# A graph network on one core: who waits for the compute engines' counters ahead of GpSimd's indirect DMAs

## The chip, the cores and the metric

One core of a Trainium2 chip. The metric is the device time of one execution in microseconds (us); times are medians of several runs. Engines: PE (TensorE), DVE (VectorE), ACT (ScalarE), POOL (GpSimd), SP (SyncE, which here only issues DMAs and waits).

## The reference

A graph with N = 50000 nodes of D = 128 features and E = 25000 directed edges, float32:

```python
h = relu(layernorm(x))
for W, b, cw, cb, a, g, be, blank in two_layers:           # sort convolution
    blank_p = W @ blank + b
    dense = up to 4 messages h[src] per node, the rest filled with blank_p
    srt = sort(dense, axis=1)                              # over the 4 slots
    o = a * h + einsum('nmd,m->nd', srt, cw) + cb
    h = h + batch_norm(o)                                  # statistics over all nodes
x = x + h
h = relu(layernorm(x))
for _ in range(5):                                         # gated graph convolution
    messages = h[col] @ W_msg.T + b_msg
    agg = segment_sum(messages, row, num_segments=N)
    h = gru(agg, h)                                        # gates r, z, n
x = x + h
```

## The kernel before, in words

Nodes are padded to NPAD = 50176, handled as NCH = 49 chunks of 1024 rows (8 per partition). Edges are sorted by target and stand as EC = 196 columns of 128. All five engines have their own program of one stage; they meet only at semaphores. Each indirect DMA (one column of 128 rows, gathered or scattered) is issued by POOL. All other DMAs of these stages are issued by SP, in the order of its program.

**Convolution** (`convolve`, once for each layer). 28 groups (NC) of seven columns (JC). POOL, in order: gather(i), seven DMAs into the ring M of four buffers (CR) (L721), then scatter(i - 3), seven DMAs out of the ring `ob` of three buffers (OR) (L729). For each group DVE masks and sorts the four slots (L818 to L847) and counts s_used and s_srt; ACT refills the blanks, moves the halo column and counts s_halo; PE mixes the sorted slots with 16 matmuls (L860) and counts s_mix; ACT adds the bias into `ob` (L784) and counts s_o. gather(i) waits for s_used and s_halo, scatter(i) for s_o. In layer 0 SP fills the second layer's output table with blank rows in 49 DMAs of 512 KB (`of`), released by s_used; in layer 1 SP has no part in the convolution.

**Statistics** (`statistics`). SP loads h (L887, 512 KB a chunk, four chunks ahead, waiting for nothing of the convolution) and the convolution's output (L893, once the scatters have landed, L892); DVE combines (L907), ACT squares (L938), PE sums over nodes with ones (L948). Beside it POOL scatters sorted columns for a later stage (L658, `pool_columns`), and waits there only for its own DMAs to land (L655).

**Second normalisation** (`apply1`). For each chunk SP loads h, o and x (L1106, L1107, L1109), three buffers deep, once DVE's L1228 three chunks back is done (s_x). DVE normalises (L2233 to L2237), adds (L1224, L1228), takes row statistics (L1235, L1240), and finishes the root and offset columns (L1209, L1211; s_row) into the ring a_r of four buffers (RR). POOL scatters the chunk to x_tab with eight DMAs (L1254) after s_row (L1250) and s_id (L1251: DVE's node number is written). Ahead of chunk NCH - 2 POOL waits for s_x and zeroes the last x buffer (L1249); SP waits for that (s_pad) before the last, partial x loads (L1111, L1113). ACT and PE compute the first step's messages in the same loop (L1129, L1137, L1144, L1156; L1174, L1181, L1184).

**Recurrent part.** Five steps; each has two halves of 49 jobs of 512 nodes. h=0: nodes without incoming edges, only their state part of the gates; beside it the gathers and the aggregation for the other half: for each group of four columns POOL gathers message rows into the ring G of four buffers (L1864), ACT builds selection matrices (L2051, L2056), PE multiplies (`tiles`, L1971; it counts s_sel), DVE adds to `agg` (L2113). h=1: nodes with edges, with the edge part of the gates (L1951, L2023). In each job DVE updates (L2164, s_d1; L2169; L2177, s_h) and evacuates the message tile (L2129, s_me) into one of two buffers m (r_m), PE makes it (`finish`, L1896). A gather waits for s_sel of four groups back (L1860). SP's order for a job: wait s_d1, load h of job k + 3 (L1753), loads and stores of the hidden parts made ahead (L1782, L1789, L1799), wait s_h, store h (L1836), store m of the job before (L1758 to L1764), in the second half of step FIN0 = 3 also the load of finished rows into a stage (L1773). In step FIN1 = 4 the first half has no jobs, only gathers, tiles and hidden parts; in the second half the result is not stored by SP: POOL puts it to the output out of r_m (L1878) after s_me. The finished half of step FIN0 is put out of the stage (L1871), where POOL waits only for the stage's load.

Of the kernel before, what the change touches and what calls it, by code (L numbers as in the profile page):

```python
# [28 lines left out]
CR = 4  # L29
# [49 lines left out]
def build(nc, x, src, dst, conv, gru, out):  # L79
# [39 lines left out]
    with ctx:  # L119
# [544 lines left out]
        def convolve(layer, c, banks, bank_read):  # L664
# [14 lines left out]
            s_sc = [stage_sem(f"{n}put{i}") for i in range(OR)]  # L679
            M0 = sb(n + "M_first", [P, 3, D], F32, c)  # L680
# [15 lines left out]
            def sync(sp):  # L696

                of = o_tab[1].rearrange("(c p t) f -> c p (t f)", p=P, t=RT)
                done = 0
                for i in range(NC):  # L700
                    sp.wait_ge(s_used, i + 1)
                    upto = NCH * (i + 1) // NC
                    for k in range(done, upto):
                        sp.dma_start(of[k], filled[1][:]).then_inc(s_fill, 16)
                    done = upto
# [8 lines left out]
            def gpsimd(pool):  # L714
                def gather(i):
                    if i >= CR:
                        pool.wait_ge(s_used, i - CR + 2)
                        pool.wait_ge(s_halo, i - CR + 2)
                    for q in range(JC):
                        j = JC * i + 3 + q  # L720
                        pool.indirect_dma_start(M[i % CR][:, 1 + q, :], None, h_tab[layer],  # L721
                                                bass.IndirectOffsetOnAxis(ap=gat_src[:, j:j + 1], axis=0)
                                                ).then_inc(s_m[i % CR], 16)

                def scatter(i):
                    pool.wait_ge(s_o, i + 1)
# [326 lines left out]
        def apply1(c, banks, spare, small, first_in):  # L1053
# [13 lines left out]
            s_pad = stage_sem("a1_pad")  # L1067
            s_w1 = stage_sem("a1_weights")
# [29 lines left out]
            def sync(sp):  # L1098
                sp.dma_start(w1[:], gru[0]).then_inc(s_w1, 16)
                for t in range(RT // 2):  # L1100
                    sp.dma_start(b1[:, t, :], gru[1].partition_broadcast(P)).then_inc(s_w1, 16)
                for i in range(NCH):
# [5 lines left out]
                    if i < NCH - 1:  # L1108
                        sp.dma_start(xb[k], xv[i]).then_inc(s_in[k], 16)  # L1109
                sp.wait_ge(s_pad, 1)  # L1110
                sp.dma_start(xb[kl][:, 0:full, :], x[m:m + full * P, :].rearrange("(t p) f -> p t f", p=P)  # L1111
                             ).then_inc(s_in[kl], 16)
                sp.dma_start(xb[kl][0:part, full, :], x[m + full * P:N, :]).then_inc(s_in[kl], 16)  # L1113

# [130 lines left out]
            def gpsimd(pool):  # L1245
                for i in range(NCH):
                    if i == NCH - 2:
                        pool.wait_ge(s_x, NCH - AR)
                        nc.gpsimd.memset(xb[kl], 0.0).then_inc(s_pad, 1)  # L1249
                    pool.wait_ge(s_row, i + 1)  # L1250
                    pool.wait_ge(s_id, 2 * i + 1)  # L1251
# [62 lines left out]
        with c:  # L1314
            banks = psum_pairs(c, "l1_ps")
            cv_vector, cv_tensor, cv_scalar, cv_gpsimd, _, _, cv_scattered, cv_free, cv_small = convolve(1, c, banks, None)
# [29 lines left out]
            @block.sync  # L1346
            def _(sp):
                st_sync(sp, cv_scattered)
                ap_sync(sp)
# [348 lines left out]
        s_op, s_oe = stage_sem("r_op"), stage_sem("r_oe")  # L1698
        c6 = ExitStack()
        with c6:  # L1700
# [46 lines left out]
            def _(sp):  # L1747
# [10 lines left out]
                def store_m(k):  # L1758
                    s, h, i = JOBS[k]
                    if h and s == FIN1:  # L1760
                        return
                    sp.wait_ge(s_me, k + 1)
# [4 lines left out]
                def staged(i):  # L1767
# [5 lines left out]
                    sp.dma_start(stg[i % 3][:].rearrange("p t f -> p (t f)"), msgv[2][i]).then_inc(s_sg[i % 3], 16)  # L1773

# [28 lines left out]
                for k, (s, h, i) in enumerate(JOBS):  # L1803
# [3 lines left out]
                    if turn and s == FIN1:  # L1807
                        for j in range(HALF + 1):
# [5 lines left out]
                            if j:  # L1814
                                store_ahead(ahead_at[s, j - 1])
                        load_kept(k)
# [26 lines left out]
                    if s == FIN0 and h:  # L1843
                        staged(i)
                for par in range(2):
# [5 lines left out]
            def _(pool):  # L1851
                nc.gpsimd.memset(zero[:], 0.0).then_inc(s_clr, 1)
                for s in range(STEPS):
# [3 lines left out]
                    for i in range(HALF):  # L1857
                        g = HALF * s + i
                        if g >= GR:
                            pool.wait_ge(s_sel, TQ * (g - GR + 1))  # L1860
# [13 lines left out]
                for i in range(HALF):  # L1874
                    k = job(FIN1, 1, i)
                    pool.wait_ge(s_me, k + 1)
# [391 lines left out]
```

## Time and profile before

| what | us |
|---|---|
| median of 3 runs | 6334.15 |
| lowest, highest | 6284.78, 6355.02 |
| span of the profiled execution | 6564.5 |

The profiled execution is one of its own, with the profiler on; its span is all of it, and it is 230 us (3.6%) longer than the median of the three unprofiled runs. Times in rows are microseconds from its start. "idle before" in square brackets is how long the instruction's engine had nothing to do ahead of it, with the instruction or engine that the profile takes for the one waited for; "issue" means that nothing is shown, "remote" that the releaser is not known. SPq are SP's DMA issues; PEld are PE's weight loads. "xN" is a count of like instructions that one row stands for.

### The profile page before, as it was taken

The numbers are of one execution on the slowest core, as the hardware profiler recorded it, in microseconds if no ns is written. First come the engines' busy times: TensorE is split into PE (matmuls) and PEld (weight loads), VectorE is DVE, ScalarE is ACT, GpSimd is POOL, SyncE is SP. The second block draws the span as 40 slices with busy tenths as digits, with TensorE's granted clock in tenths as the row PEclk, the third lists the DMA queues.
The fourth block names the chain that finished last, engine by engine and source line by source line (L and its number), as shares of the span: only waits on it lengthen the run. The fifth ranks groups of instructions, "written<-read, shape, count | busy, mean of one in ns | idle before, by whom it ended". The sixth has DMA issues, their size and how long they took to land. (4 is left out here: it accounts for less than half of the span.)

```text
span 6564.5 us, 61506 instructions
## 1 busy us (share of the span) xinstructions
PE 4257.9 (65%) x15022; PEld 2341.7 (36%) x15022; DVE 3845.9 (59%) x7518; ACT 2733.4 (42%) x5325; POOL 3376.4 (51%) x3399
## 2 busy tenths in 40 slices
PE   8944352602344754343577899789889978884586
PEld 5612121300121333232344455455445544442333
DVE  8965530397564255564466676667667756652265
ACT  6822210222222134343476654664465456433432
POOL 8766677046666434544665600640262056556666
PEclk9966676855666877677799999999999999997699
DMA  6722231694111585654476654664465456664444
GB/s 217 256 97 88 80 117 46 238 307 153 40 41 38 195 246 164 179 170 132 140 205 192 213 183 138 201 199 166 150 217 193 138 187 202 214 189 135 123 144 145
DMA packets 628093, 1062.87 MB, mean 162 GB/s; under 512 B 105048, under 2 KB 258158, under 8 KB 627740
## 3 DMA queue, kind: packets, MB, share of 16 engines
q1 hardware_dynamic: 498972, 818.46, 38.6%
q0 software_dynamic: 100544, 163.41, 9.0%
q10 hardware_dynamic: 28224, 77.08, 3.0%
q8 instruction: 126, 2.06, 0.1%
q14 instruction: 227, 1.86, 0.1%
HBM read 599.34 MB, written 464.81 MB: 162 GB/s over the span
## 5 line engine op out<-in xcount | busy, mean ns | idle before, releaser
L1864 POOL DMA_INDIRECT r_G<-msg_tab,srow x784 | 739.6, 943 | 1324.9 <-DMA msg_tab<-r_m 895.0
L860 PE MATMUL l_ps<-cv_V,cv_cwi 128*128 128x448 f32 x896 | 478.3, 702 | 916.7 <-ACT cv_ob L784 457.4
L1254 POOL DMA_INDIRECT x_tab<-a_r,node_pos x392 | 379.6, 968 | 514.7 <-DVE a_r L1211 246.7
L860 PEld LDWEIGHTS l_ps<-cv_V,cv_cwi 128*128 128x128 f32 x896 | 220.4, 253 | 1174.7 <-issue 1161.6
L2113 DVE TENSOR_TENSOR agg<-r_psS,agg 128x128 f32 x980 | 281.7, 287 | 514.7 <-DMA st_o<-o_tab 324.7
L729 POOL DMA_INDIRECT o_tab<-cv_ob,put_idx x392 | 387.7, 989 | 271.9 <-ACT cv_ob L784 147.8
L1945 PE MATMUL r_psR<-r_hin,whh 128*128 128x512 f32 x882 | 463.5, 608 | 27.3 <-ACT r_r L2066 11.4
L1896 PEld LDWEIGHTS r_psM<-wmsg,r_hnew 128*128 128x128 f32 x2744 | 355.8, 195 | 339.5 <-DVE r_hnew L2177 219.1
L1896 PE MATMUL r_psM<-wmsg,r_hnew 128*128 128x128 f32 x2744 | 384.0, 284 | 133.4 <-DVE r_hnew L2177 126.2
L721 POOL DMA_INDIRECT cv_M<-h_tab,gat_src x392 | 373.9, 954 | 119.5 <-issue 119.5
L1181 PE MATMUL l_ps<-a_bmsg,row 128*128 128x512 f32 x196 | 152.5, 871 | 429.3 <-ACT cv_M L1137 271.6
L907 DVE SCALAR_TENSOR_TENSOR st_o<-st_h,ab,st_o 128x1024 f32<-128x1024 f32 x98 | 125.9, 1285 | 507.9 <-DMA st_o<-o_tab 453.2
L784 ACT ACTIVATE cv_ob<-l_ps,cbb 128x896 f32<-128x896 f32 x56 | 56.4, 1007 | 817.5 <-remote 670.4
L948 PE MATMUL l_ps<-st_q,ones 128*128 128x512 f32 x384 | 213.0, 683 | 211.4 <-issue 181.1
L1917 PE MATMUL r_psR<-r_oin,whh 128*128 128x512 f32 x290 | 189.4, 740 | 245.5 <-issue 156.0
L658 POOL DMA_INDIRECT sort_tab<-pair,sort_at x196 | 195.6, 998 | 277.6 <-DVEq L1040 214.1
L1945 PE MATMUL r_psZ<-r_hin,whh 128*128 128x512 f32 x642 | 330.4, 596 | 11.9 <-issue 3.9
L818 DVE COPY_PREDICATED l_ps<-l_ps,cv_M 128x896 f32<-128x896 int32 x56 | 61.5, 1099 | 452.3 <-ACT cv_M L762 399.7
L2129 DVE TENSOR_TENSOR r_m<-r_psM,bmsg 128x512 f32<-128x512 f32 x343 | 235.7, 687 | 150.7 <-remote 80.3
L938 ACT ACTIVATE st_q<-st_o 128x1024 f32<-128x1024 f32 x98 | 103.3, 1056 | 514.5 <-remote 168.6
L1971 PE MATMUL r_psS<-r_sel,r_G 128*128 128x128 f32 x1960 | 293.0, 298 | 28.2 <-DMA r_G<-msg_tab,srow 17.7
L2051 ACT ACTIVATE r_dist<-iota_w,lrank 128x128 f32<-128x128 f32 x980 | 310.0, 390 | 0.0
(292 smaller groups left out, 11307.7 us busy)
## 6 DMA issues: line engine op xcount, KB each, us to landing
r_hin<-ht_tab SPq DMA_DIRECT2D x441, 256.0 KB
msg_tab<-r_m SPq DMA_DIRECT2D x392, 256.0 KB
ht_tab<-r_hnew SPq DMA_DIRECT2D x343, 256.0 KB
o_tab<-o_blank SPq DMA_DIRECT2D x98, 512.0 KB, 6.0
st_h<-h_tab SPq DMA_DIRECT2D x98, 512.0 KB
st_o<-o_tab SPq DMA_DIRECT2D x98, 512.0 KB
r_oin<-ht_tab SPq DMA_DIRECT2D x161, 256.0 KB
i_x<-x_tab SPq DMA_DIRECT2D x49, 528.0 KB
```

Of the source, the lines that this page charges most:

```text
L721: pool.indirect_dma_start(M[i % CR][:, 1 + q, :], None, h_tab[layer], bass.IndirectOffsetOnAxis(ap=gat_src[:, j:j + 1], axis=0)).then_inc( ...
L729: pool.indirect_dma_start(o_tab[layer], bass.IndirectOffsetOnAxis(ap=put_idx[:, j:j + 1], axis=0), ob[i % OR][:, q, :], None, bounds_check ...
L860: ins = nc.tensor.matmul(psO[:, h, 0:HW], cwi[m][:], V[i % 2][m][:, HW * h:HW * (h + 1)], start=m == 0, stop=m == 3)
L948: ins = nc.tensor.matmul(ps, w[:], t[:, 512 * q:512 * (q + 1)], start=i == 0 and q == 0, stop=i == NCH - 1 and q == 1, skip_group_check=True)
L1254: pool.indirect_dma_start(x2_tab, bass.IndirectOffsetOnAxis(ap=node_pos[:, j:j + 1], axis=0), rb[i % RR][:, t, :], None).then_inc(s_out[i ...
L1864: pool.indirect_dma_start(G[g % GR][:, q, :], None, msg_tab[s % 3] if s else first_tab, bass.IndirectOffsetOnAxis(ap=at, axis=0)).then_inc ...
L1896: ins = nc.tensor.matmul(psM[:, t, :], hnew[k % 2][:, P * t:P * (t + 1)], wmsg[:], start=True, stop=True)
L1945: ins = nc.tensor.matmul(ps, whh[:, g * D:(g + 1) * D], hin[k % 3][:], start=True, stop=not edges)
L1971: nc.tensor.matmul(psS[g % 2][:, q, :], G[g % GR][:, q, :], sel[g % 2][:, q, :], start=True, stop=True).then_inc(s_sel, 1)
L2051: nc.scalar.activation(dist[:, q, :], iota_w[:, 0:SW], ACT.Abs, bias=lrank[:, TQ * i + q:TQ * i + q + 1]).then_inc(s_di, 1)
L2113: nc.vector.tensor_tensor(agg[:, bass.ds(at[q], SW)], psS[g % 2][:, q, :], agg[:, bass.ds(at[q], SW)], ALU.add).then_inc(s_ev, 1)
L2129: nc.vector.tensor_tensor(mb[k % 2][:], psM[:], other, ALU.add).then_inc(s_me, 1)
```

## The change

Three kinds of edit, with two new semaphores for the convolution and one or two for the other stages. Ahead of its indirect DMAs POOL no longer waits for counters of DVE, ACT or PE; SP waits for these and increments a semaphore of its own for which POOL waits. In the convolution SP's loop runs over NC + OR rounds and its fills stand three groups later; it now runs in layer 1 too, ahead of the statistics' loads (in both layers these follow the whole loop). In `apply1` chunk i is passed on behind the loads of chunk i + 4, the last four behind or around the last two loads; the zeroing of the last x buffer stands one chunk earlier. In the recurrent part the pass for the gathers stands at the end of a job's work on SP, and `store_m` waits for s_me in the last half too and passes it on there.

```diff
             def sync(sp):
                 of = o_tab[1].rearrange("(c p t) f -> c p (t f)", p=P, t=RT)
                 done = 0
-                for i in range(NC):
-                    sp.wait_ge(s_used, i + 1)
-                    upto = NCH * (i + 1) // NC
+                for i in range(NC + OR):
+                    if CR <= i < NC:
+                        sp.wait_ge(s_used, i - CR + 2)
+                        sp.wait_ge(s_halo, i - CR + 2)
+                        sp.sem_inc(s_open, 1)
+                    if i >= OR:
+                        sp.wait_ge(s_o, i - OR + 1)
+                        sp.sem_inc(s_ready, 1)
+                    upto = NCH * max(0, i + 1 - OR) // NC if layer == 0 else 0
                     for k in range(done, upto):
                         sp.dma_start(of[k], filled[1][:]).then_inc(s_fill, 16)
                     done = upto
...
                 def gather(i):
                     if i >= CR:
-                        pool.wait_ge(s_used, i - CR + 2)
-                        pool.wait_ge(s_halo, i - CR + 2)
+                        pool.wait_ge(s_open, i - CR + 1)
...
                 def scatter(i):
-                    pool.wait_ge(s_o, i + 1)
+                    pool.wait_ge(s_ready, i + 1)
```

```diff
+                def send(i):
+                    sp.wait_ge(s_row, i + 1)
+                    sp.wait_ge(s_id, 2 * i + 1)
+                    sp.sem_inc(s_send, 1)
+
                 for i in range(NCH):
...
                     sp.dma_start(ob[k][:], ov[i]).then_inc(s_in[k], 16)
                     if i < NCH - 1:
                         sp.dma_start(xb[k], xv[i]).then_inc(s_in[k], 16)
+                    if i >= 4:
+                        send(i - 4)
+                send(NCH - 4)
                 sp.wait_ge(s_pad, 1)
...
                 sp.dma_start(xb[kl][0:part, full, :], x[m + full * P:N, :]).then_inc(s_in[kl], 16)
+                for i in range(NCH - 3, NCH):
+                    send(i)
...
             def gpsimd(pool):
                 for i in range(NCH):
-                    if i == NCH - 2:
+                    if i == NCH - 3:
                         pool.wait_ge(s_x, NCH - AR)
                         nc.gpsimd.memset(xb[kl], 0.0).then_inc(s_pad, 1)
-                    pool.wait_ge(s_row, i + 1)
-                    pool.wait_ge(s_id, 2 * i + 1)
+                    pool.wait_ge(s_send, i + 1)
```

```diff
             @block.sync
             def _(sp):
+                cv_sync(sp)
                 st_sync(sp, cv_scattered)
                 ap_sync(sp)
```

```diff
                 def store_m(k):
                     s, h, i = JOBS[k]
+                    sp.wait_ge(s_me, k + 1)
                     if h and s == FIN1:
+                        sp.sem_inc(s_send, 1)
                         return
-                    sp.wait_ge(s_me, k + 1)
...
+                def summed(g):
+                    sp.wait_ge(s_sel, TQ * (g + 1))
+                    sp.sem_inc(s_gopen, 1)
...
                             if j:
                                 store_ahead(ahead_at[s, j - 1])
+                            if 1 <= j < HALF:
+                                summed(HALF * s + j - 1)
...
                     if s == FIN0 and h:
                         staged(i)
+                    if h == 0 and i:
+                        summed(HALF * s + i - 1)
+                    if h and i == 0:
+                        summed(HALF * s + HALF - 1)
+                store_m(len(JOBS) - 1)
...
                         if g >= GR:
-                            pool.wait_ge(s_sel, TQ * (g - GR + 1))
+                            pool.wait_ge(s_gopen, g - GR + 1)
...
                 for i in range(HALF):
                     k = job(FIN1, 1, i)
-                    pool.wait_ge(s_me, k + 1)
+                    pool.wait_ge(s_send, i + 1)
```

## Rows read from the trace of the kernel before

**Rows 1.** The page's section 1: busy us (share of the span) and instructions by engine.
```profile
PE 4257.9 (65%) x15022; PEld 2341.7 (36%) x15022; DVE 3845.9 (59%) x7518; ACT 2733.4 (42%) x5325; POOL 3376.4 (51%) x3399
```

**Rows 2.** Windows: start:end, length, busy us (count) by engine; PEclk, DMA share, GB/s.
```profile
2370.00:3124.00 754.00, 307.75 (x1351) 216.99 (x1351) 438.12 (x1224) 308.85 (x680) 380.57 (x393) 0.70 0.57 167
3505.00:3810.00 305.00, 254.63 (x1114) 150.00 (x1115) 199.13 (x433) 198.61 (x416) 185.46 (x197) 0.97 0.66 205
3810.00:4090.00 280.00, 278.00 (x941) 148.09 (x940) 197.75 (x300) 130.64 (x200) 0.00 (x0) 0.99 0.46 155
```

**Rows 3.** Waits of POOL, whole span: tile, line <- releaser: us in total, times, longest.
```profile
POOL x_tab L1254 <- DVE a_r L1211: 246.7, 17, 16.1
...
POOL r_G L1864 <- DMA st_o<-o_tab: 219.3, 146, 4.2
...
POOL o_tab L729 <- ACT cv_ob L784: 147.8, 23, 8.5
...
POOL out_dram L1878 <- DVE r_m L2129: 69.6, 19, 21.7
```

**Rows 4.** Timeline, second convolution: start, us, instruction, [idle before <- releaser].
```profile
1709.53 9.19 PE L860 MATMUL l_ps<-cv_V,cv_cwi 128*128 128x448 f32 x16 [6.79 <-issue]
...
1735.10 0.94 POOL L721 DMA_INDIRECT cv_M<-h_tab,gat_src  x1 [0.30 <-issue]
1742.09 1.01 ACT L784 ACTIVATE cv_ob<-l_ps,cbb 128x896 f32<-128x896 f32 x1 [29.22 <-remote]
...
1743.90 1.01 POOL L729 DMA_INDIRECT o_tab<-cv_ob,put_idx  x1 [7.86 <-ACT cv_ob L784]
```

**Rows 5.** Waits in the stretch 911 to 1165, first statistics.
```profile
ACT st_q L938 <- remote: 148.7, 8, 21.4
```

**Rows 6.** Waits in the stretch 5600 to 5935, second half of the fourth step.
```profile
ACT r_r L2085 <- remote: 55.2, 12, 10.0
```

**Rows 7.** Timeline of one round of the second normalisation.
```profile
2436.05 0.17 DVE L1211 SCALAR_TENSOR_TENSOR a_r<-a_mv,a_r 128x8 f32<-128x8 f32 x1
...
2436.50 0.97 POOL L1254 DMA_INDIRECT x_tab<-a_r,node_pos  x1 [11.79 <-DVE a_r L1211]
2436.96 1.17 SPq L1109 DMA_DIRECT2D cv_high<-in_x_dram  x1
...
2437.77 0.97 POOL L1254 DMA_INDIRECT x_tab<-a_r,node_pos  x1 [0.30 <-issue]
```

**Rows 8.** Timeline of one period in the first half of a recurrent step.
```profile
3602.68 0.68 DVE L2177 TENSOR_TENSOR r_hnew<-r_psHN,r_d 128x512 f32<-128x512 f32 x1
...
3604.41 1.06 PE L1971 MATMUL r_psS<-r_sel,r_G 128*128 128x128 f32 x8
...
3607.66 0.29 DVE L2113 TENSOR_TENSOR agg<-r_psS,agg 128x128 f32 x1 [1.53 <-DMA st_o<-o_tab]
3607.80 0.94 POOL L1864 DMA_INDIRECT r_G<-first_tab,sorted  x1 [1.30 <-DMA st_o<-o_tab]
...
3608.66 0.68 DVE L2177 TENSOR_TENSOR r_hnew<-r_psHN,r_d 128x512 f32<-128x512 f32 x1
...
3609.37 0.32 SPq L1836 DMA_DIRECT2D ht_tab<-r_hnew  x1
...
3609.73 0.44 SPq L1764 DMA_DIRECT2D msg_tab<-r_m  x1
```

**Rows 9.** Timeline at the last puts.
```profile
6247.90 0.69 DVE L2129 TENSOR_TENSOR r_m<-r_psM,r_x 128x512 f32<-128x512 f32 x1 [1.65 <-DMA r_x<-x_tab]
...
6248.51 0.68 DVE L2164 TENSOR_TENSOR r_d<-r_hin,r_psHN 128x512 f32<-128x512 f32 x1
...
6249.42 1.01 POOL L1878 DMA_INDIRECT out_dram<-r_m,ids  x1 [21.67 <-DVE r_m L2129]
```

**Rows 10.** Timeline at the start of the second layer's convolution and statistics.
```profile
1548.66 4.94 SPq L887 DMA_DIRECT2D st_h<-h_tab  x4
...
2138.12 1.28 DVE L907 SCALAR_TENSOR_TENSOR st_o<-st_h,ab,st_o 128x1024 f32<-128x1024 f32 x1 [25.86 <-DMA st_o<-o_tab]
```

More of the change, by code:

```diff
@@ L679, in convolve @@
             s_sc = [stage_sem(f"{n}put{i}") for i in range(OR)]
+            s_open = stage_sem(n + "buffer_open")
+            s_ready = stage_sem(n + "rows_ready")
             M0 = sb(n + "M_first", [P, 3, D], F32, c)
@@ L1067, in apply1 @@
             s_pad = stage_sem("a1_pad")
+            s_send = stage_sem("a1_send")
             s_w1 = stage_sem("a1_weights")
@@ L1315, in build @@
             banks = psum_pairs(c, "l1_ps")
-            cv_vector, cv_tensor, cv_scalar, cv_gpsimd, _, _, cv_scattered, cv_free, cv_small = convolve(1, c, banks, None)
+            cv_vector, cv_tensor, cv_scalar, cv_gpsimd, cv_sync, _, cv_scattered, cv_free, cv_small = convolve(1, c, banks, None)
             st_vector, st_tensor, st_scalar, st_gpsimd, st_sync, st_in = statistics(1, c, banks, sort_tab, sort_at, pair,
@@ L1698, in build @@
         s_op, s_oe = stage_sem("r_op"), stage_sem("r_oe")
+        s_gopen, s_send = stage_sem("r_gather_open"), stage_sem("r_send")
         c6 = ExitStack()
```

## The prediction

> **What bounds the kernel now.** I read the page's busy times first: no engine is full over the span, PE is busy for 4257.9 us and POOL for 3376.4 of 6564.5 [rows 1], so the order of the work decides, stage by stage. The windows come next: in the first half of a recurrent step POOL issues 197 indirect DMAs and is busy for 185.46 us of 305, in the second half none in 280, with PE busy for 278.00 [rows 2]. Then POOL's waits, the rows that the change is aimed at: 147.8 us over 23 waits ahead of the scatters of both convolutions, 246.7 over 17 in the second normalisation, 219.3 over 146 ahead of the recurrent gathers, 69.6 over 19 ahead of the last puts [rows 3]. (The gathers' row names a DMA; by the code this wait is on PE's count of tiles, so I read the row as a misnamed releaser.)
>
> A wait on POOL's row costs time only if the one waited for was late for its own reasons. So I looked at one such place in time order. In the second convolution PE's group of 16 matmuls starts at 1709.53 and ends 9.19 later, at 1718.72. ACT, which waits for exactly that, starts its rows at 1742.09, after 29.22 of idle; POOL's last gather ended at 1736.04; POOL goes on at 1743.90 [rows 4]. For 23.4 us PE's increment was not seen, while POOL issued one DMA behind the other with 0.30 between; it came 6.05 us after POOL stopped. The three engines run in such cycles: a blind stretch as long as POOL's work in hand, then a few us in which everybody moves. The change can be of use only if this lateness comes from POOL's waiting on a compute engine's counter. Two stretches speak against that. In the first statistics stage POOL scatters too, and waits there for DMA counters only: ACT waits 21.4 us, eight times, 148.7 in all [rows 5]. In the second half of the fourth step POOL's puts wait only for a DMA's counter by the code, and ACT's wait for PE is still up to 10.0 us, 12 times [rows 6]. So the lateness goes with POOL's issuing, which the change leaves as it is: the same 7 or 8 or 4 DMAs in a row.
>
> One page would explain part of it by the way it is recorded. The Trainium skill ("Perfetto Trace Analysis", Per-engine timelines) says that TensorE's end is estimated from the instruction's size. The rows don't allow it for the bulk: ACT's start at 1742.09 is no PE end, and 23 us is more than twice the whole group [rows 4].
>
> **Convolutions.** Removed from POOL: two counter waits ahead of each gather from the fifth group on, one ahead of each scatter; added: one relayed wait for each. SP does nothing else in these stages but layer 0's 49 fills, so the relay costs one hop. A hop is seen in the recurrent part: DVE's add ends at 3609.34 and SP's transfer starts at 3609.37 [rows 8], 0.03 us. With the increment itself I take 0.08 for each of 23 waits: 23 × 0.08 = 2 us. Bounds: 0, and POOL's own way from ACT's end at 1743.10 to 1743.90 paid twice [rows 4], 23 × 0.80 = 18. The fills come three groups later and end with the convolution instead of before it; they feed only the second layer. The four loads of the statistics' first chunks are no longer issued early (1548.66, 4.94 us of SP [rows 10]) but behind SP's last relay, some 10 us before the first loads of the other operand; DVE starts on both at 2138.12 [rows 10]. That cover is thin, since 2 MB more are then in flight; I take 1.5 for each layer, +3, with bounds of 0 and 2 × 4.94 = 10.
>
> The same page speaks against any relay: a sequencer's semaphore step has a hidden tail, its propagation to the other engines is in no profiled window (the Trainium skill, "Perfetto Trace Analysis", Sequencer-only Instruction). "Advanced Engine Details and Errata", Network/Comms, in the Trainium skill gives 50 to 100 ns for a sequencer's read of a semaphore; 23 of those would be 1 to 2 us, by estimate the same sum.
>
> **Second normalisation.** SP passes chunk i on only after it has issued chunk i+4's three loads. At 2436.50 POOL starts on a chunk after 11.79 us of waiting for DVE's L1211 at 2436.05; SP's loads of that round run until 2436.96 + 1.17 = 2438.13 [rows 7]. The relay would open some 0.4 us after that, 2.0 later than now. That hits the rounds in which POOL waits: 17 × 2.0 = 34 us of POOL's time. Of chunk time it is less: eight DMAs of POOL are 8 × 1.27 = 10.2 us by the spacing of its starts (2436.50, 2437.77 [rows 7]), of 754/49 = 15.4 for a chunk [rows 2], and its tiles come free a whole chunk before DVE needs them. What it delays is when the blind stretch starts, and DVE gains the same time ahead of it. I take +2 for that and +3 for the end, where the last three relays stand behind the two last loads: +5. Bounds: 0 and 49 × 2.0 = 98. The memset's wait on DVE's counter stays, one group earlier.
>
> **Recurrent part, first halves.** SP relays behind the stores of the job: now the gather starts at 3607.80, L2177 ends at 3609.34, SP's two stores start at 3609.37 and 3609.73 and end by 3610.17 [rows 8]. So the relay opens 3610.17 − 3607.80 = 2.4 us later than POOL's wait does, 2.6 with a hop and an increment. PE reads this gather four periods behind the tiles that ended at 3605.47, from about 3605.47 + 4 × 5.98 − 1.06 = 3628.3 on, 20.5 us after its first DMA. The four DMAs take 4.7 to issue; if their landing took twice that again, 6 us would be left, and 2.6 of these go: nothing is late. What moves is the phase. PE's tiles end at 3605.47 and are added by DVE only at 3607.66, 1.16 us after POOL's fourth gather ended (3607.80 − 1.30 = 3606.50); the period is 3608.66 − 3602.68 = 5.98 [rows 8], against 280/49 = 5.71 in the half without gathers [rows 2]. If a later burst left PE's increments alone, 49 × 5 × 0.27 = 66 us would be gained; if it met the tiles' end 2.6 later in each period, DVE's slack of 35% of 5.98 (busy 199.13 of 305 [rows 2]) would take 2.1 of it, and 0.5 × 245 = 122 would be lost. Nearest to the row is that the cycle locks again to the end of the burst, one period being one burst: 0.
>
> **Last puts.** POOL starts at 6249.42, 0.83 after DVE's L2129 ended; SP's relay stands behind its wait for L2164, which ends at 6249.19 [rows 9], so 0.6 to 0.7 later. Both m buffers are then free later: 19 × 0.7 = 13 at most, 0 where PE and DVE are ahead; +2.
>
> **Sum:** 2 + 3 + 5 + 0 + 2 = +12 on the profiled execution, 6564.5 → 6576. That execution is 230 us longer than the median of the three runs, 6334.15, most likely in these same blind stretches, which differ from run to run; a term of 12 doesn't change by 3.6%. Forecast: 6334 + 12 = **6346 us**, own range 6300 to 6395. (About 1% is what a measurement of this kernel can tell from no change.)
>
> **Rivals.**
> A, faster: POOL's waiting on a compute counter is what holds increments back. For it: the waits of 147.8 and 246.7 are long and come just at these places [rows 3], and ACT's 29.22 ends when POOL's own wait begins [rows 4]. Price: 147.8 + 246.7 + 66 = 460 of the profile; half of it is 230, and gives 6104. Against it: rows 5 and 6. Chance 0.18. A weaker form, in which only the phase of the recurrent bursts is better: −66, 6268. Chance 0.12.
> B, slower: SP's order. [...] It decides where POOL's wait is on the path in each round, above all in the second normalisation: 49 × 2.0 = 98, 6432. For it: POOL there waits for DVE in 17 rounds [rows 3], and with SP in its loads at that moment [rows 7]. Against: eight DMAs are 10.2 of 15.4. The recurrent loss of 122 belongs here too (6456). Chance 0.24.
> C, the change doesn't do what it says: the memset still waits for a compute counter, and for the rest only the name of the counter changes; POOL waits as long, for the same engines' work at one remove. That is the forecast's own case: 0 to +12.
>
> **How the numbers follow.** Forecast 0.36 and C 0.10, together 0.46 within 1%. A 0.18 and its weaker form 0.12: 0.30 faster by over 1%. B: 0.24 slower by over 1%. Downwards the range reaches to 6150, which is the weaker form and 40% of A's 460 (6334 − 184); upwards over B's 6432, to 6440. Left out are A at its half and more, some 0.12, and B with both losses, 0.08.
>
> **What would show it.** Right: ACT's rows in the convolutions still wait above 20 us for PE, every third group; POOL's waits keep their sums of some 148 and 247 but name SP or an unknown; the period of the first halves stays at 5.98, with the gather 2.5 later in it; statistics start within 3 us as now. A would show as ACT starting within 1 us of PE's end while POOL issues, and as chunks of under 14.5 us. B would show as POOL's starts tied to the end of SP's loads, with chunks of 16.5 us and more. The forecast is wrong if a convolution stage changes by more than 10 us, or the second normalisation (754, rows 2) by more than 15.

## The result, and the profile after

| | us |
|---|---|
| before, median of 4 runs | 6344.59 (6284.78 to 6468.83) |
| after, median of 4 runs | 6600.64 (6589.59 to 6614.71) |
| ratio | 1.0425, 95% interval 1.0382 to 1.0467 |
| span of the profiled execution, before and after | 6564.5, 6608.5 |

The ratio leaves out runs more than 1.5% above a kernel's fastest (here the one of 6468.83, in one later session 14 of the 23 of the kernel before), so medians of all runs stand beside it, and it is these that I compare.

The change makes the kernel 256 us slower by these medians. The two profiled executions are only 44 us apart: the one of before happened to be 220 above its median, the one of after 8. So the profiles alone explain 44, and the rest had to be found in what differs between executions.

Windows of the profile after (start:end, length, busy by engine, PEclk, DMA share, GB/s): the second normalisation and the first half of a recurrent step.

```profile
2379.00:3065.00 686.00, 314.54 (x1335) 223.79 (x1336) 426.31 (x1219) 309.59 (x678) 381.59 (x393) 0.70 0.62 182
3455.00:3795.00 340.00, 273.02 (x1113) 172.05 (x1113) 199.46 (x433) 197.75 (x416) 185.42 (x196) 0.89 0.58 183
```

Against [rows 2] the normalisation is shorter (754 to 686) and the first half of a step longer (305 to 340), with the same work in it. Part of that is PE itself: its 1113 matmuls are busy for 273.02 us in place of 254.63, at a mean granted clock of 0.89 of full speed in place of 0.97. By POOL's first and last gather in the timeline the first three steps take 329.8, 335.4 and 332.8 us where they took 291.4, 292.2 and 291.8: 38.4, 43.2 and 41.0 more, 123 in all. The fourth is unchanged (298.9 before, 299.1 after). The sends of the normalisation, second to last chunk, spread over 653.0 instead of 725.0. The convolutions differ by 8 us each, downwards.

POOL's waits after, whole span:

```profile
POOL r_G L1895 <- SPq L1797: 368.1, 116, 7.7
POOL x_tab L1271 <- SPq L1113: 335.6, 19, 168.7
...
POOL o_tab L736 <- SPq L709: 134.2, 23, 7.9
```

The waits ahead of the scatters (134.2 over 23) and the puts (51.3 over 11) answer to [rows 3] with another name, as forecast. The gathers' are fewer and longer. In the first step they look so, before (3520 to 3790) and then after (3500 to 3780), each with the wait of ACT's gate in the same stretch:

```profile
POOL r_G L1864 <- DMA st_o<-o_tab: 51.0, 37, 3.4
...
ACT r_r L2066 <- PE r_psR L1945: 17.0, 38, 1.6
```

```profile
POOL r_G L1895 <- SPq L1797: 73.0, 21, 4.7
...
ACT r_r L2097 <- remote: 48.7, 16, 3.9
```

Half as many waits mean that the bursts pair up. I counted DMAs of POOL with at most 1.1 us between them as one burst: besides an opening one of 16 or 20, in each of the first three first halves the kernel before has 40 to 42 bursts of four gathers and one or two of eight, the kernel after 20 or 21 of eight and two to four of four. In the fourth step both kernels are mixed, 13 of eight and 18 of four before, 14 and 16 after, and take the same time. One pair of periods of the first step, after (timeline: start, us, instruction, idle before):

```profile
3599.15 1.02 PE L1976 MATMUL r_psR<-r_hin,whh 128*128 128x512 f32 x2
...
3600.83 0.95 POOL L1895 DMA_INDIRECT r_G<-first_tab,sorted  x1 [0.30 <-issue]
3603.55 0.69 ACT L2097 ACTIVATE r_r<-r_psR,brz 128x512 f32<-128x512 f32 x1 [3.76 <-remote]
...
3605.30 2.07 PE L1927 MATMUL r_psM<-wmsg,r_hnew 128*128 128x128 f32 x8 [4.27 <-DVE r_hnew L2208]
...
3606.40 0.95 POOL L1895 DMA_INDIRECT r_G<-first_tab,sorted  x1 [4.62 <-SPq L1797]
```

In [rows 8] a burst of four gathers ran over the end of the tiles, whose adds had room, and then POOL stopped for 1.3 us. Now eight gathers run from 3592.07 to 3601.78 with 0.30 between, and their last ones lie over PE's state part (3599.15 to 3600.17). ACT's gate, which waits for that, starts at 3603.55, 1.77 us after the burst's last DMA ended (3601.78), and the whole chain behind it (gate, h, PE's next m at 3605.30 after 4.27 of idle) is late. These eight matmuls then take 2.07 us, where the same eight took 1.16 in the kernel before (at 3603.41): the granted clock is 0.50 (1.2 GHz) from 3603.05 to 3609.87, after PE's idle stretch, and was 1.00 (2.4 GHz) all through this period before.

Not every increment of PE is late while POOL issues. In the kernel before PE's message tile ends at 3604.57, in the third DMA of a burst, and DVE starts on it at 3604.62; it is the tiles' end at 3605.47 that DVE sees only after the burst.

Second normalisation, after:

```profile
2437.27 0.17 DVE L1229 SCALAR_TENSOR_TENSOR a_r<-a_mv,a_r 128x8 f32<-128x8 f32 x1
...
2438.18 1.37 SPq L1122 DMA_DIRECT2D cv_high<-in_x_dram  x1
...
2439.90 0.97 POOL L1271 DMA_INDIRECT x_tab<-a_r,node_pos  x1 [4.12 <-SPq L1113]
```

POOL starts 2.46 us after DVE's columns are done (0.28 in [rows 7]), so the relay costs the 2.0 that was forecast, and yet the stage is shorter.

The second statistics stage, 2132 to 2379 in the profile before, has late increments too, which the prediction doesn't mention. ACT's squares wait there up to 20.7 us until POOL's stream of some 70 DMAs is issued:

```profile
ACT st_q L938 <- DMA st_o<-o_tab: 70.7, 7, 20.7
```

The profile after has the same (20.6), so the difference of the two profiles doesn't contain it.

### The profile page after: what moved, and what is told of

The parts are those of the page before. It is cut to its first block and busy times, and to the rows that moved or that the text cites. A ratio compares the mean times of both kernels' runs of the same rounds, so it can differ in the third digit from the quotient of the medians.

```text
span 6608.5 us, 61856 instructions
## 1 busy us (share of the span) xinstructions
PE 4337.0 (66%) x15022; PEld 2430.8 (37%) x15022; DVE 3841.8 (58%) x7518; ACT 2736.7 (41%) x5325; POOL 3379.1 (51%) x3399
## 5 line engine op out<-in xcount | busy, mean ns | idle before, releaser
L1927 PE MATMUL r_psM<-wmsg,r_hnew 128*128 128x128 f32 x2744 | 406.9, 296 | 188.6 <-DVE r_hnew L2208 183.2
L1927 PEld LDWEIGHTS r_psM<-wmsg,r_hnew 128*128 128x128 f32 x2744 | 388.8, 208 | 379.4 <-DVE r_hnew L2208 244.9
L736 POOL DMA_INDIRECT o_tab<-cv_ob,put_idx x392 | 388.6, 991 | 254.7 <-SPq L709 134.2
L2002 PE MATMUL r_psS<-r_sel,r_G 128*128 128x128 f32 x1960 | 328.5, 323 | 27.5 <-DMA r_G<-msg_tab,srow 16.6
L2002 PEld LDWEIGHTS r_psS<-r_sel,r_G 128*128 128x128 f32 x1960 | 305.5, 237 | 81.3 <-issue 59.8
L1938 PE MATMUL r_psHN<-r_hin,whh 128*128 128x512 f32 x560 | 314.1, 645 | 7.1 <-DMA r_hin<-ht_tab 7.1
```

The lines of the kernel that those rows point to most:

```text
L736: pool.indirect_dma_start(o_tab[layer], bass.IndirectOffsetOnAxis(ap=put_idx[:, j:j + 1], axis=0), ob[i % OR][:, q, :], None, bounds_check ...
L1927: ins = nc.tensor.matmul(psM[:, t, :], hnew[k % 2][:, P * t:P * (t + 1)], wmsg[:], start=True, stop=True)
L1938: nc.tensor.matmul(psHN[k % 2][:], whh[:, 2 * D:3 * D], hin[k % 3][:], start=True, stop=True).then_inc(s_hn, 1)
L2002: nc.tensor.matmul(psS[g % 2][:, q, :], G[g % GR][:, q, :], sel[g % 2][:, q, :], start=True, stop=True).then_inc(s_sel, 1)
```

## The experiments

Seven sessions, each kernel beside the kernel before on one chip. The chips fall in two kinds: on three the kernel before takes 5514 or 5515 us, on four 6421 to 6551 (and 6345 on that of the result). I call the second kind "late chips", for what the profile of e1 shows below. Each chip was seen in one session only, so "chip" here always means the chip in that session.

| experiment | edit | kernel before | median | ratio (95%) |
|---|---|---|---|---|
| e1_gather_only | gathers' relay alone | 5515 | 5512.7 | 0.9994 (0.9985 to 1.0004) |
| e2_norm_only | normalisation's relay alone | 5515 | 5510.4 | 0.9988 (0.9977 to 0.9998) |
| e3_conv_only | convolutions' part alone | 5515 | 5519.0 | 1.0009 (0.9999 to 1.0019) |
| e4_all_but_gather | all but the gathers' relay | 5515 | 5520.3 | 1.0006 (0.9996 to 1.0016) |
| e5_whole_again | the whole change | 5515 | 5523.1 | 1.0016 (1.0005 to 1.0026) |
| e6_gather_again | as e1 | 5515 | 5513.4 | 0.9998 (0.9989 to 1.0008) |
| e7_direct_late | later wait, no relay | 6421 | 6624.4 | 1.0311 (1.0270 to 1.0352) |
| e8_gather_third | as e1 | 6421 | 6585.7 | 1.0241 (1.0198 to 1.0284) |
| e9_all_but_gather_again | as e4 | 6551 | 6557.8 | 1.0149 (1.0087 to 1.0211) |
| e10_conv_again | as e3 | 6551 | 6596.8 | 1.0233 (1.0175 to 1.0290) |
| e11_h_late | h loads late, nothing else | 6518 | 6553.0 | none |
| e12_conv_h_early | e3 with early h loads | 6518 | 6453.8 | 0.9964 (0.9858 to 1.0070) |
| e13_norm_again | as e2 | 6518 | 6478.5 | none |
| e14_pause | stops beside the statistics | 6531 | 6419.6 | 0.9993 (0.9952 to 1.0035) |
| e15_pause_norm | e14 and e2 | 6531 | 6387.5 | 0.9978 (0.9950 to 1.0007) |
| e16_whole_pause | e14 and the whole change | 6531 | 6558.2 | 1.0232 (1.0179 to 1.0284) |
| e17_conv_stop | e15 and stops in the convolutions | 5514 | 5686.8 | 1.0315 (1.0301 to 1.0329) |
| e18_pause_norm_again | as e15 | 5514 | 5578.1 | 1.0116 (1.0101 to 1.0132) |

**The parts, one at a time (e1 to e6).** e1, the core of its edit:

```diff
-                            pool.wait_ge(s_sel, TQ * (g - GR + 1))
+                            pool.wait_ge(s_gopen, g - GR + 1)
```

with `summed` and its calls on SP as in the change; e2, e3 and e4 take the change's lines of their stages as they are.

> Of the change only the relay ahead of the recurrent gathers. Theory 1 (phase: the later burst of four gathers now runs while PE finishes what the gates wait for): nearly all of the loss is here, the first halves of steps 0 to 2 take 330 to 336 us instead of 292, and the time is 150 to 300 above the kernel before (ratio 1.025 to 1.047). Theory 2 (every relay costs, through SP's order): a third of the loss at most, ratio under 1.015.

> Of the change only the second normalisation's relay. Theory 1: that stage is faster, sends spread over 640 to 670 us instead of 725, ratio 0.985 to 1.000 (1.000 if the kernel before has its slow stage only in the profiled execution). Theory 2: slower, ratio above 1.005.

> Of the change only the convolutions' part. Theory 1: within 0.4% of the kernel before; the profile's convolutions differ by under 10 us each. Theory 2: slower by 0.5 to 1.5%.

> The whole change, but the recurrent gathers wait for PE's counter themselves again. Theory 1: the loss is gone, ratio 0.98 to 1.005, first halves of steps 0 to 2 at 292 us. Theory 2: most of the loss stays, ratio above 1.02.

> The whole change once more. The runs of its parts stood beside a kernel before of 5515 us, not 6344, and on that chip ACT starts 0.04 us after PE's end in the convolutions where it had waited up to 23 us. Theory 1 (the loss needs the late increments): where the kernel before takes about 5515, ratio 0.998 to 1.003; where it takes about 6340, ratio 1.03 to 1.05. Theory 2 (the parts add up to a loss only together, whatever the chip): ratio above 1.02 also at 5515.

> Only the recurrent gathers' relay, once more. Theory 1: at a kernel before of 5515 ratio 1.00 as in the first run of it; at 6340 ratio 1.03 to 1.05, with first halves of steps 0 to 2 of 330 us or more. If the loss at 6340 comes from the other parts instead, ratio 0.99 to 1.01 there.

All are within 0.2% of the kernel before, beside 5515 us. The whole change costs 8 us there. e1 missed what theory 1 said of it; e2, e3 and e4 lie within theirs, which says little on a chip that shows no loss at all; e5 came out as its theory 1 had it, so the chip decides. The profile of e1 shows what is absent on such a chip. Second convolution, PE's mixing and ACT's rows (timeline):

```profile
1467.15 9.33 PE L860 MATMUL l_ps<-cv_V,cv_cwi 128*128 128x448 f32 x16 [9.88 <-DVEq L847]
...
1476.52 1.01 ACT L784 ACTIVATE cv_ob<-l_ps,cbb 128x896 f32<-128x896 f32 x1 [7.53 <-PE l_ps L860]
```

and the first half of the first recurrent step (window):

```profile
2830.00:3077.00 247.00, 242.09 (x1112) 150.73 (x1112) 194.46 (x431) 200.44 (x415) 184.71 (x196) 0.98 0.79 252
```

ACT starts 0.04 us after PE's end, with POOL issuing its DMAs in the same 1.25 to 1.3 us rhythm; in [rows 4] it was 23.4. It is 0.04 in all 56 groups of both convolutions of e1, while 33 of the 56 in the kernel before are over 1 us, up to 27.8. A half step takes 247 us, not 305. So late increments come with the chip (or with how it was set up in that session), not with the kernel, and without them the whole change costs 0.16% (e5). The 0.04 also says that the modelled end of PE, which the prediction put aside with the Trainium skill's "Perfetto Trace Analysis", Per-engine timelines (TensorE's end is estimated from the instruction's size), is no source of the lateness.

**The relay or its moment (e7, e8), on a late chip.** e7 leaves the relay out and takes only its later moment:

```diff
                             pool.wait_ge(s_sel, TQ * (g - GR + 1))
+                            sb_, ib = divmod(g - GR, HALF)
+                            if sb_ < FIN1:
+                                kb = job(sb_, 0, ib + 1) if ib + 1 < HALF else job(sb_, 1, 0)
+                                pool.wait_ge(s_h, kb + 1)
+                                pool.wait_ge(s_me, kb)
```

> The kernel before, but each recurrent gather also waits, on GpSimd itself, for the h (s_h) and the m (s_me) behind which SyncE would pass it on; nothing is relayed. Theory 1 (phase): where the kernel before takes about 6340, this is as slow as the relay, ratio 1.03 to 1.05, since the burst of gathers starts as late in the job. Theory 3 (it is the relay itself, GpSimd waiting on SyncE's counter): ratio 0.99 to 1.01. Where the kernel before takes about 5515, both say 0.998 to 1.002.

> Only the gathers' relay, beside e7_direct_late on the same chip. Theory 1: the same ratio as e7_direct_late within 0.01, above 1.03 where the kernel before takes 6340. Theory 3: above 1.03 there, with e7_direct_late at 1.00. At 5515 both 1.00.

Ratios 1.0311 and 1.0241, the second below the 1.03 that was expected; in medians of all runs 204 and 165 us. The first halves of steps 0 to 2 take 349.8, 349.9 and 346.9 us in e7, 349.1, 352.0 and 350.1 in e8. Theory 3 falls: GpSimd waiting itself, on a compute counter, is as slow as the relay once it waits for the same moment. The gathers pair up in the same way, 21 bursts of eight in the first half step of both e7 and e8. POOL's waits in e7, 3400 to 3700:

```profile
POOL r_G L1869 <- DVE r_hnew L2182: 84.0, 19, 5.4
```

So it is the later moment that makes the pairs. Through which step it does was not isolated. The fourth step of e11, a run whose recurrent part is that of the kernel before, shows that it needs no relay: 17 bursts of eight there, and 331 us in place of 299.

**What the other parts do on a late chip (e9, e10).**

> The whole change but for the gathers' relay, in the hope of a chip on which the kernel before takes 6300 to 6450. There: theory 1 (the gathers' phase makes the loss, the normalisation's relay gains some 70): ratio 0.98 to 0.995, first halves at 292 us. Theory 4 (the convolutions' part tips the first statistics stage into its long form in every run: 281 us where a short one takes about 110): ratio 1.00 to 1.02. At a before of 5515: 1.000 to 1.002.

> Only the convolutions' part. Where the kernel before takes 6300 to 6450: theory 1 says ratio 0.995 to 1.005 and both forms of the first statistics stage in the runs, some 150 us apart; theory 4 says every run has the long form, ratio 1.015 to 1.03. At a before of 5515: 1.000 to 1.002.

The first halves of steps 0 to 2 are back at 291 to 294 us, so all of the recurrent loss belongs to the gathers. But e9 misses the 0.98 to 0.995 of theory 1, being slower than the fast half of the kernel before's runs, and all 6 runs of e10, the convolutions' part alone, lie above 6500 (median 6596.8), as theory 4 had it. In e10's profile the convolutions are as before (578.0 against 577.9 for the second, 567.4 against 572.5 for the first); the stretch between them, with the first statistics, takes 653, as in the profile before. The same stretch took 485 in e7. How it comes about is in the profile after; ACT's squares in the first statistics stage, each with its wait:

```profile
921.03 1.06 ACT L945 ACTIVATE st_q<-st_o 128x1024 f32<-128x1024 f32 x1 [2.38 <-issue]
927.17 1.06 ACT L945 ACTIVATE st_q<-st_o 128x1024 f32<-128x1024 f32 x1 [5.09 <-remote]
943.96 1.06 ACT L945 ACTIVATE st_q<-st_o 128x1024 f32<-128x1024 f32 x1 [15.73 <-remote]
966.36 1.06 ACT L945 ACTIVATE st_q<-st_o 128x1024 f32<-128x1024 f32 x1 [21.34 <-remote]
```

The wait starts at 2.38, climbs within a few chunks to 21.34 and stays there until POOL's stream of gathers is issued (L661 before, 196 DMAs). Some executions escape the climb: in e7 the wait stays at 3.6 and less through the same unbroken stream, and that is worth 168 us. In e8 the climb begins only after some 20 chunks, and the stretch takes 611. I call the ends a long and a short form of the stage.

The second statistics stage has them too. By its squares, first to last, it takes 219 to 229 us in six late traces (before, after, e7, e8, e9, e13) and 164 to 166 in six (e10, e11, e12, e14, e15, e16), some 60 less; on the other chips it takes 165. So the time of one execution depends on two stages, each with a form of its own.

On late chips 29 of the 57 runs of the kernel before lie above 6500 us (none of the four of the result); of the 18 of e9, e10 and e11, 17 do.

**Why it climbs more often (e11, e12).** e11 is the kernel before plus one line at the end of SP's convolution loop, and e12 is e3 with the four h loads issued ahead of the last three rounds:

```diff
+                sp.wait_ge(s_o, NC)
```

```diff
                     done = upto
+                    if i == NC - 1 and between:
+                        between(sp)
```

> The kernel before with one wait more: SyncE issues the first statistics stage's four h loads only after the last s_o, as the change does; no relay, fills as before. Theory 4a (the late h loads tip that stage into its long form): where the kernel before takes 6300 and more, every run long, above 6500. Theory 4b (it is not the loads but the rest of the convolutions' part, the late fills or the relay): both forms, a third to a half of the runs short, under 6500. At a before of 5515: 1.000 to 1.001.

> The convolutions' part of the change, but with the four h loads issued ahead of the last three relays and fills, where the kernel before has them. Theory 4a: both forms among the runs, as in the kernel before. Theory 4b: every run long, above 6500. At a before of 5515: 1.000 to 1.002.

e11: 5 of 6 runs above 6500. e12: 3 of 6, and 6 of 11 for the kernel before beside them. That leans to theory 4a (the late h loads), whose "every run" failed. Alone e11 proves little: in its session early loads give 9 of 17 above 6500. With the session of e9 and e10, late loads give 17 of 18 and early ones 16 of 28, which chance would make in under 1% of cases; but 12 of the 18 also have the relays and the late fills. So the late loads are the likelier cause and not a shown one, and through which step they tip the stage was not seen.

> Only the second normalisation's relay. Theory 1: where the kernel before takes 6300 and more, 50 to 75 us faster form for form (ratio 0.985 to 0.995), its sends spread over 650 to 685 us instead of 721 to 725. If that gain needs other parts of the change, ratio 1.00. At a before of 5515: 0.998 to 1.000, as measured there.

e13 has six runs from 6358 to 6554, median 6478.5 beside 6517.7 (39 less, where 50 to 75 was expected), and its sends spread over 656.3 us: the gain in the sends is real by itself, how much of it arrives can't be read from runs that scatter over 200. The traces say more. From the last scatter of the second convolution to the first recurrent gather, with the long form of the second statistics, it takes 1375, 1407 and 1397 us without this relay (before, e7, e8) and 1325, 1344 and 1378 with it (after, e13, e9); with the short form 1328 to 1333 without (e10, e11, e12, e14) and 1306 and 1303 with it (e15, e16). So some 25 us arrive beside the short form; beside the long one the traces scatter too much to tell.

**A short stop (e14 to e16).** In the column DMAs beside the statistics (`pool_columns`) every group of 14 now waits for the group before it:

```diff
+                if i >= 1 and first:
+                    pool.wait_ge(s_done[(i - 1) % 2], 16 * JG * ((i - 1) // 2 + 1))
```

> The kernel before, with a pause for GpSimd: in the column scatters and gathers beside the statistics (L658, L661) each group of 14 waits until the group before it has landed, so GpSimd stops for some 2 us after every 14 DMAs. Theory 5 (compute increments pile up while GpSimd issues without a gap, and a short stop lets them through): where the kernel before takes 6300 and more, no run has the long first statistics stage (no ACT wait above 18 us in it), all runs within 6250 to 6450, ratio to its short runs 0.97 to 1.00. Theory 6 (a stop that short clears nothing): both forms as before, and the pauses cost 10 to 40 us. At a before of 5515: 1.00 to 1.01, slower if anything.

> e14_pause with the second normalisation's relay: 45 to 75 us below e14_pause on a chip where the kernel before takes 6300 and more; at 5515 within 10 us of it.

> The whole change with the same pause. If theory 5 holds and the change's loss is the gathers' phase plus the long statistics stage, the second goes: 6400 to 6500 where the whole change alone has 6600, and e16 minus e15 is the recurrent part's 120 to 170. If the pause clears nothing, 6590 and more.

Theory 5 held: all 12 runs of e14 lie between 6391 and 6445, where the kernel before beside it has 13 of 23 above 6500. Same stretch, 911 to 1165, in the kernel before and in e14 (windows):

```profile
911.00:1165.00 254.00, 90.25 (x146) 36.69 (x147) 25.32 (x20) 19.02 (x18) 192.73 (x196) 0.66 0.25 75
```

```profile
911.00:1165.00 254.00, 170.35 (x392) 75.14 (x392) 140.40 (x119) 68.44 (x66) 171.24 (x160) 0.84 0.83 295
```

ACT makes 66 operations in it instead of 18. And where [rows 5] has eight waits of up to 21.4 us from an unknown releaser, the waits of e14 there are

```profile
ACT st_q L940 <- PE l_ps L950: 75.2, 32, 3.3
```

POOL's stops in it come to

```profile
POOL look L663 <- DMA look<-node_tab,src_at: 35.2, 10, 4.3
```

35 us of waiting, and 45 over the whole stage (13 stops, the longest 5.9). The stretch between the convolutions takes 536 us in e14, against 653 in the long form and 485 in the short one. The stops cost 51 beside the short form and save 117 beside the long. The second statistics stage, which has the stops too, is short in all three traces of e14 to e16. A stop waits until the DMAs have landed, so it ends POOL's issuing and its DMAs' traffic at once; which of the two holds the increments back wasn't separated. e15 takes 32 us less than e14, not the 45 to 75 expected: its sends spread over 673.9 instead of 723.4, but the first gather of the recurrent part comes only 24 us earlier after the convolution (1307.4 instead of 1331.6), as the stage's end follows another chain. e16 missed its 6400 to 6500 (all six runs lie above 6549). Against e15 it has the change's recurrent part and its convolutions' part: 6558.2 − 6387.5 = 171 us; first halves of 352.9, 353.8 and 351.7 against 291.9, 294.2 and 293.8, together 178.5. On this pair the gathers' later moment explains the whole difference, and it costs more for each half step than on the chip of the result (60 against 41).

e15 is the version to have on a late chip: 144 us (2.2%) below the kernel before's median of all runs. It is no faster than the fast runs of the kernel before (0.9978); what it gains is that no run is slow.

**What it costs elsewhere (e17, e18).** e17 adds the same kind of stop to the convolutions:

```diff
+                    if OR <= i < NC:
+                        pool.wait_ge(s_m[i % CR], 16 * JC * (i // CR + 1))
                     if i >= OR:
                         scatter(i - OR)
```

> e15_pause_norm with a stop in the convolutions too: ahead of each scatter GpSimd waits until the gather that it has just issued has landed, about 2 us in every 18. Theory 5: where the kernel before takes 6300 and more, ACT's waits of 29 us for PE in the convolutions fall under 12, the stop costs GpSimd 28 x 2 us in each layer and saves about as much: within 40 us of e18 either way. Theory 6 (there a short stop clears nothing): e18 plus 80 to 120 us. At a before of 5515, where GpSimd bounds the convolutions: 80 to 120 us slower than e18.

> e15_pause_norm again, beside e17_conv_stop. Where the kernel before takes 6300 and more: median 6370 to 6410, all runs within 50 us. At a before of 5515: 5505 to 5540, since the pauses gain nothing there.

The session fell on a chip without late increments. e18 costs 64 us there (5578.1, ratio 1.0116), where 5505 to 5540 was expected: the stretch between the convolutions takes 76 us more than in e3. e17 costs 109 more, as expected: 54 and 56 us in the two convolutions. Whether a stop frees the convolutions on a late chip wasn't measured.

## Why the prediction was wrong

**"The lateness goes with POOL's issuing, which the change leaves as it is"**: the first half held: e7 has no relay and the same loss, and in the profile after, where POOL waits for no compute counter, ACT still waits 21.34 us. With that rival A falls. The second half is where the reasoning broke: the change doesn't leave the bursts as they are, it makes eights of the fours. (For rival A the prediction also read that ACT's 29.22 ends when POOL's wait begins; by [rows 4] it ends 6.05 us later, as the prediction itself says further up.)

**"Nearest to the row is that the cycle locks again to the end of the burst, one period being one burst: 0"** is the step that failed, in the recurrent part. The relay opens later as computed (POOL starts 1.15 us after h is done where it started 1.54 ahead of it, 2.7 against the 2.6 forecast), and no wait of PE's tiles for a gather shows. But two periods now share one burst of eight: POOL stops 21 times for 73.0 us where it stopped 37 times for 51.0, the end of the burst covers PE's increments for the gate, and each first half loses some 41 us. The bound beside it, "0.5 × 245 = 122 would be lost", has the size that the profile shows (123 over three steps; 171 in medians on another chip, e16 against e15). That is luck: it rested on DVE's slack, which isn't the mechanism, its 245 periods count a fifth first half that has no jobs, and the fourth step, with the same relay, loses nothing.

**First statistics, "That cover is thin", +3**: the edit was named and its size missed. If the late loads are what tips the stage (likely, not shown), the price isn't the time of four loads but the step from one form to the other, up to 168 us. The row that showed the long form was on the table ([rows 5], eight waits of up to 21.4 us, 148.7 in all, which the prediction read as 21.4 eight times) and so was the sign that it isn't always so: a profiled execution 230 us above the median. The prediction wrote "most likely in these same blind stretches" and "a term of 12 doesn't change by 3.6%". It should have asked which form the median has, and what tips it. Of the 256 us, 44 is the difference of the profiles, in which the gathers' 123 and 13 in the first statistics stand against a normalisation that is 49 us shorter end to end, 16 in the convolutions and some 27 in the later steps; 168 is the form of the first statistics that the profile of before had and most of its four timed runs seem not to have had. The second statistics stage can account for the rest: both profiles have its long form, some 55 us above the short one without the relay (247 us against 192 in e10, from the last scatter to the first send). By estimate from these traces, a run of the kernel before with both short forms takes 6564.5 − 168 − 55 = 6342 us, beside a median of 6344.59. The timed runs have no traces, so this isn't shown.

**Second normalisation, "2.0 later"**: right (2.46 against 0.28 after DVE's columns, 2.2 more), and the sign of the sum was wrong: +5 forecast, 72 shorter by its sends. In the kernel before POOL sends three chunks without a gap and then waits, mostly 15.4 us, 17 waits in all; after, it waits 19 times with a median of 8.4. In e9, e13 and e15, with the same relay, it waits 16 times with a median of 11.0 to 11.7. So what the relay brings everywhere is a shorter wait, and not more of them. Why it is shorter wasn't isolated, and less arrives at the stage's end than the sends gain (49 us after, 24 in e15 against e14).

**Convolutions, 2 us of hops**: within the error (e3: 1.0009). **Last puts, +2**: the bound of 13 is what the profiles on chips without late increments show: by DVE's updates the last second half takes 266.4 and 266.7 us with the relay (e5, e4), 253.7 to 256.5 without. On the chip of the result it became 12 shorter.

**Rival B** (slower, 6432 or 6456) had the sign and, with its "recurrent loss of 122", the right half steps, but named SP's order as the cause; e7 shows that SP needn't be there. Its range ended at 6440 since the losses were never added to a change of form.

## What to carry to other kernels

A wait that is moved later moves the work behind it too: ask whether the bursts stay apart and what they will lie over, not only whether their data comes in time. When the profiled execution is hundreds of us away from the median, suspect a kernel with more than one form, and a change is worth what it does to their frequency as well as to their terms. And measure on more than one chip before deciding: here one change is 4.3% slower on one and 0.2% on another, and the remedy (e15, a stop for GpSimd after every 14 DMAs, with the normalisation's relay) gives 2.2% in the median on one and costs 1.2% on another.

## What the runs showed of the hardware

- Chips differ: the same kernel takes 5514 to 5515 us on three (the sessions of e1, e5 and e17) and 6345 to 6551 on five, with POOL busy for much the same time (3396 us in e1, 3376 in the profile before). In e1 ACT starts 0.04 us after PE's end in all 56 groups of the convolutions; in the profile before 33 of 56 starts are over 1 us late, up to 27.8.
- On late chips some increments of PE are seen late while GpSimd issues indirect DMAs without a gap: 1.2 us after the end of a burst of four (3607.66 in [rows 8]), 1.8 us after one of eight, 6.05 us after a longer one, and in a stream of over a hundred the wait climbs from 2.4 over 5 and 16 to 21.3 us. Not all are late: DVE starts 0.05 us after PE's end in the third DMA of a burst, 23 of the 56 groups in the profile before are within 1 us, and in e7 a stream of 196 leaves the wait at 3.6 and less.
- In e14 to e16, with a stop after every 14 DMAs (3.5 us on average, at most 5.9 in e14), no trace has the long form of either statistics stage; ACT waits for PE 3.3 us at most in the stretch of e14 shown.
- It makes no difference that could be told for whom GpSimd waits, a compute engine's counter or SyncE's (e7 and e8: 1.031 and 1.024, intervals that overlap).
- Where increments are prompt, a relay over SyncE that stands behind nothing cost nothing that could be measured (e3: 1.0009, interval from 0.9999), nor did the gathers' (e1: 0.9994). The last puts' relay cost 10 to 13 us there (e4, e5). The Trainium skill ("Perfetto Trace Analysis", Sequencer-only Instruction) puts the propagation of a sequencer's semaphore step outside what a profile shows; if it cost anything here, it is within the 0.2% by which e1 and e3 could differ from the kernel before.
